# Three low parts of h made by GpSimd instead of VectorE in a split-precision graph kernel

## The reference

```python
h = maximum(layernorm(x, axis=-1), 0)          # (32, 256, 1024)
fv = h.mean(axis=1); nf = fv / norm(fv)        # graph from the column means
A  = adjacency(top_k(outer(nf, nf), 9)[1:])    # symmetric, ones on the diagonal, 1024 x 1024
t  = relu((A / deg) @ (h.T @ W1.T + b1))       # W1 = adj (256 x 256)
t  = (A / deg) @ (t @ W2.T + b2)               # W2 = adj as well
out = x + t.T
```

## Time and profile before

| | us |
|---|---|
| median of 3 runs | 477.64 (476.87 to 478.04) |
| the profiled execution | 475.69 |
| its span, first to last instruction | 473.9 |
| around the span | 1.79 |
| PE, DVE, ACT, POOL busy | 421.5, 395.6, 307.8, 220.9 |
| mean granted clock of TensorE | 0.986 of 2.4 GHz |

### The profile page before, as it was taken

How to read it: one execution, slowest core, us unless ns; L and a number is a source line. 1 busy time by engine, 2 the same in 40 slices (tenths; PEclk the granted TensorE clock), 3 DMA queues, 4 the chain that set the end, 5 groups by cost and what they waited for, 6 DMA issues and landing times.

```text
span 473.9 us, 7615 instructions
## 1 busy us (share of the span) xinstructions
PE 421.5 (89%) x2220; PEld 176.2 (37%) x2220; DVE 395.6 (83%) x682; ACT 307.8 (65%) x657; POOL 220.9 (47%) x937
## 2 busy tenths in 40 slices
PE   0653898999978799899999999899999999999996
PEld 0121343334323344344443443344434444344432
DVE  5999898988897998999899998999899828854463
ACT  2979687989766777667777769667766843014400
POOL 2536656374736435552737454744656253415200
PEclk9995999999999999999999999999999999999999
DMA  8990000159202493065703590078404400341026
GB/s 295 382 410 29 1 0 2 44 223 340 107 0 94 174 326 119 1 262 175 273 3 132 205 355 21 0 268 284 160 0 179 177 2 0 142 160 55 0 94 262
DMA packets 19401, 68.21 MB, mean 144 GB/s; under 512 B 1824, under 2 KB 2464, under 8 KB 19360
## 3 DMA queue, kind: packets, MB, share of 16 engines
q1 hardware_dynamic: 19360, 67.73, 38.2%
HBM read 34.17 MB, written 33.55 MB: 143 GB/s over the span
## 4 chain that ended last, share of the span: by engine, by line
DVE 39%; PE 31%; ACT 11%; issue 9%; POOL 7%; DMA 1%; POOLq 1%; SPq 0%; DVEq 0%; ACTq 0%
PE ps L451 26%; DVE hl L1109 9%; DVE hl L1118 7%; DVE bn L1087 7%; DVE xs L1134 5%; ACT hl L663 4%; ACT hf L654 4%; PE ps L457 3%; ACT hl L675 2%; DVE fv L1150 2%; DVE idx L1158 2%; POOL gat L876 2%; PE pm L506 1%; DMA xs<-x_dram 1%; POOL nw L858 1%
## 5 line engine op out<-in xcount | busy, mean ns | idle before, releaser
L451 PE MATMUL ps<-hl,wh 128*128 128x512 f16 x896 | 268.7, 382 | 20.6 <-DVE wl L1293 11.3
L451 PE MATMUL ps<-hl,wl 128*128 128x512 f16 x448 | 170.5, 381 | 0.0
L451 PEld LDWEIGHTS ps<-hl,wh 128*128 128x128 f16 x896 | 83.9, 99 | 131.4 <-issue 22.0
L654 ACT ACTIVATE hf<-xs,nbias,rstd 128x1024 f32<-128x1024 f32 x64 | 79.2, 1237 | 25.3 <-POOL nbias L862 17.4
L1109 DVE TENSOR_TENSOR hl<-hf,hl 128x1024 f16<-128x1024 f32 x64 | 76.9, 1211 | 15.5 <-ACT hl L663 15.3
L1134 DVE SCALAR_TENSOR_TENSOR xs<-ps,sc,xs 128x1024 f32<-128x1024 f32 (+1 forms) x71 | 78.9, 1137 | 5.9 <-PE ps L457 5.9
L1118 DVE SCALAR_TENSOR_TENSOR hl<-ps,hl 128x1024 f16<-128x1024 f32 (+1 forms) x55 | 57.2, 1083 | 20.3 <-ACT hl L675 20.2
L675 ACT ACTIVATE hl<-ps 128x512 f16<-128x512 f32 x96 | 55.7, 594 | 22.0 <-PE ps L457 22.0
L663 ACT ACTIVATE hl<-hf 128x1024 f16<-128x1024 f32 x64 | 67.6, 1056 | 2.0
L1087 DVE BATCH_NORM_STATS2 bn<-xs 128x6 f32<-128x512 f32 x96 | 61.2, 678 | 5.0 <-DMA xs<-x_dram 5.0
L451 PEld LDWEIGHTS ps<-hl,wl 128*128 128x128 f16 x448 | 44.0, 98 | 53.5 <-issue 1.1
(11 more groups left out here) (146 smaller groups left out, 537.6 us busy)
## 6 DMA issues: line engine op xcount, KB each, us to landing
xs<-x_dram SPq DMA_DIRECT2D x62, 512.0 KB, 7.4
out_dram<-xs SPq DMA_DIRECT2D x31, 1024.0 KB, 5.1
xs<-x_dram SPq DMA_DIRECT2D x4, 256.0 KB, 3.7
out_dram<-xs SPq DMA_DIRECT2D x4, 256.0 KB, 2.1
wt<-adj_t_dram SPq DMA_DIRECT2D x1, 256.0 KB, 9.8
b1r<-b_row_dram SPq DMA_DIRECT2D x1, 128.0 KB, 9.3
b2r<-b_row_dram SPq DMA_DIRECT2D x1, 128.0 KB, 10.8
cs<-consts_dram SPq DMA_DIRECT2D x1, 84.5 KB, 9.6
```

Of the source, the lines that this page charges most:

```text
L451: pe.matmul(bank(i, e), w[:, k, o], src, start=(k == 0 and w is wh and part == 0), stop=False)
L654: act.activation(hf[:, c % NHF], xs[:, n % NX, k], ACT.Relu, bias=nbias[:, n % RB, k:k + 1], scale=rstd[:, n % RB, k:k + 1], accum_out=s_a ...
```

## The change

The subtraction that makes the low part goes to GpSimd for three of the 64 chunks: (4, 1), that is batch 4, k = 1, then (5, 0) and (8, 0). The first two belong to group 1 and stand ahead of the first class rows, the third behind them. They are taken out of VectorE's list. Since `lo_ready` counts chunks and two engines now add to it, GpSimd waits until the chunk before is counted, and VectorE does so where the chunk before was GpSimd's.

```diff
+        ON_POOL = ((4, 1), (5, 0), (8, 0))
...
+            def pool_lo(n, k):
+                c = KC * n + k
+                pool.wait_ge(hi_ready, c + 1)
+                pool.wait_ge(lo_ready, c)
+                pool.tensor_tensor(hl[:, n % NHL, 1, k], hf[:, c % NHF], hl[:, n % NHL, 0, k], ALU.subtract
+                                   ).then_inc(lo_ready, 1)
...
             for n in range(6):
                 coefs(n)
+            pool_lo(4, 1)
             for b in batches(0):
                 gather(b)
             plain_q1(0)
+            pool_lo(5, 0)
             coefs(6)
             class_q1(0)
...
             late_sums(0)
+            pool_lo(8, 0)
             for b in batches(1):
                 gather(b)
...
                 dve.wait_ge(hi_ready, c + 1)
+                if ((c - 1) // KC, (c - 1) % KC) in ON_POOL:
+                    dve.wait_ge(lo_ready, c)
...
             kinds(0)
-            h_lo(4, 1)
             top_sums(0)
...
-            h_lo(5, 0)
             y_lo(*unit(0, 0)[1:])
             y_lo(*unit(0, 1)[1:])
...
             final(*unit(0, 11)[1:])
-            h_lo(8, 0)
             final(*unit(0, 12)[1:])
```

## The result

The changed kernel takes 480.5 us (median of 12 runs, 479.1 to 481.8) where the kernel before took 477.1 beside it (12 runs, 475.5 to 478.5). The ratio is 1.0082, with a 95% interval of 1.0068 to 1.0097: slower by 3.9 us, 3.2 to 4.6. The two medians alone differ by 3.4 us, which lies inside that interval. The profiled execution took 480.66 us, its span 478.9.

The account below looks back on a forecast made before the run. PE was busy for 89% of the span, but only the first two groups' handover, chained through GpSimd, counted. 2.75 + 1.35 - 0.1 + 0.6 = +4.6 us made 475.69 into 480.3, as median 482.2 us; range 479.4 to 484.2.

Parts of the forecast that it names:

- Term A: At chunk (4, 1): GpSimd waits for (4, 0), then subtracts, so gathers and VectorE's sum come late; +2.75 us.
- Term B: At chunk (5, 0): VectorE, making `cr`, stands until GpSimd's subtraction ends, so `lw` is late and PE waits; +1.35 us.
- Rival (1): At `cr` and layer 2's rows: VectorE is not held by GpSimd's long read; +2.5 us, 480.1 us; chance 0.24.
- The removal of (5, 0): VectorE no longer runs this chunk, but its next step needs ScalarE's read of the unit; -0.1 us.
- Term C: At chunk (8, 0): VectorE held at layer 2's rows, +0.8, less 0.2 gained behind the gathers; +0.6 us.
- Rival (2): PE's clock falls in the new gap before the first class rows; +0.9, in all +5.5 us, 483.1 us; chance 0.16.

Follow-up runs that it names:

- e4_mid41: The changed kernel with (4, 1) moved behind two of the four gathers of group 0, all three chunks still on GpSimd; 479.0 us, ratio 1.0059.
- e2_only50: The change cut to chunk (5, 0) alone on GpSimd, the other two back on VectorE; 477.3 us, ratio 1.0014 to the kernel before.
- e6_pieces50: Chunk (5, 0) alone on GpSimd, as eight subtractions of 128 columns instead of one; 476.7 us, ratio 1.0002 to the kernel before.
- e8_80late: Chunk (8, 0) alone on GpSimd, started only when `lw` of layer 2 is written; 476.2 us, ratio 0.9998 to the kernel before.
- e7_41filler: Chunk (4, 1) alone on GpSimd, with twelve unused matmuls filling PE's stop ahead of `plain_rows(0)`; 479.1 us, ratio 1.0044 to the kernel before.
- e3_only80: The change cut to chunk (8, 0) alone on GpSimd, the other two back on VectorE; 477.2 us, ratio 1.0005 to the kernel before.
- e1_only41: The change cut to chunk (4, 1) alone on GpSimd, the other two back on VectorE; 480.5 us, ratio 1.0080 to the kernel before.
- e5_filler: The changed kernel with twelve unused matmuls filling PE's stop ahead of `plain_rows(0)`; 481.3 us, ratio 1.0085 to the kernel before.
- e9_steady: The kernel before, with one chunk in each of groups 2 to 6 on GpSimd, behind `class_q1`; 474.5 us, ratio 0.9937.
- e11_two80: e10 with chunk (8, 0) also on GpSimd, started behind `lw` of layer 2 of group 0; 472.0 us, ratio 0.9903 to the kernel before.
- e10: e9_steady with a second chunk on GpSimd in groups 2 to 5, ahead of `late_sums`; 471.6 us, ratio 0.9887 to the kernel before.

## Why the prediction was right

**Term A**, 2.75 us by the prediction, measured 2.36. The order of events was as told: GpSimd stood for chunk (4, 0), then subtracted, then copied. The price was 2.13 us (2.1 predicted, from rows of 8 and 96 elements). What was too large is the stretch from there to the end of the gathers: 1.23 for the kinds and four batches of 1.23 make 6.15 us to the end of the last `hu` row, and it took 5.68 (46.18 to 51.86), a batch taking 1.17 and the kinds holding the copies for 1.0. e4_mid41 splits the term: 1.42 us are the place ahead of the gathers, 0.94 the work itself, less what GpSimd no longer stands for.

**Term B**, 1.35, measured 1.14 to 1.17. Rival (1), that VectorE is not held, is out: e2_only50 shows it standing until the subtraction ends, and e6_pieces50 shows that the hold goes with GpSimd's running instruction. The step was wrong in the instruction that stands. It is the TENSOR_SCALAR of 128x64, one tensor as input, ahead of the TENSOR_TENSOR that the prediction named. The section of the Trainium skill that the prediction cited (SBUF — State Buffer, "Who interferes with whom") covers this case as well: it counts `tensor_scalar` among the instructions that can enter a mode with both ports and then contend, when their operands meet certain conditions. The long row of `cr` agrees with it (1.45 for 0.26 us), and the two long rows with two inputs agree with what the prediction cited (2.10 for 1.23, 1.11 for 0.47 us). That this instruction ran in such a mode is what the page would say; the runs show only that it stood.

**The removal of (5, 0)**, -0.1, was worth 0.03 (1.17 at `lw`, 1.14 behind it): ScalarE is the cover, as said; VectorE waits 1.23 us for it there.

**Term C**, +0.6, measured 0.45 to 0.5. The hold of line 1242 was 0.64 us (0.8 predicted), shown by its absence in e8_80late. The time that is won when VectorE doesn't run (8, 0) was there too, 0.49 us, but it is worth nothing at the end, where the prediction gave it 0.2. The prediction misread its source: of the copies' delay only the 0.30 us of 1.38 against 1.08 came from (8, 0), and the idle time ahead of them (1.09) is still 1.06 in e8_80late, without it. What it missed is the wait that takes the gain up: e8_80late has it at PE until `plain_rows(1)`, and loses it where VectorE waits for ScalarE's `kind`, as the changed kernel also does (0.35 us).

**Rival (2), the clock,** came true beside the forecast and not instead of it. The prediction had it cost 0.9 us; it cost 0.5 in the whole change and 1.67 with (4, 1) alone. That A and B were 0.6 us smaller than told and the clock 0.5 us dearer is why the first class rows came 4.04 us late where 4.1 was forecast: that agreement is chance. It also means that the costs don't add: (4, 1) alone and the whole change are equally late there, since PE at half its clock covers what (5, 0) costs. The fall of this first clock was seen in the one profile that each of the two kernels has.

**The end.** The parts alone, from e7_41filler, e2_only50 and e3_only80, make 2.37 + 1.14 + 0.5 = 4.0 us without the clock, 4.5 with its first fall; the runs give 3.9 (3.2 to 4.6) and can't choose between them. The forecast was 4.6 over the profiled execution. Its median of 482.2 is 1.7 above the 480.5 measured: 0.7 of that is 4.6 for 3.9, 0.6 is that the kernel before had a median of 477.64 in three runs and of 477.1 in twelve beside the change, and the rest is that the two medians are only 3.4 us apart. So 480.5 as a number is nearer to rival (1)'s 480.1 than to the forecast; against rival (1) stand the held rows, and the 3.9 us (3.2 to 4.6) measured side by side, where it had 2.5.

**What stays open.** The second fall of the clock, at 135 to 142. It is seen in five profiles (the change, e1_only41, e5_filler, e9_steady, e11_two80) and not in e2, e3, e4, e6, e7, e8 and e10, behind a stop of PE of about 2.1 us there that the kernel before has too (2.15 us), with its clock kept in its profile. It cost the change 1.05 us in the profile and is no part of the 4.0. Being late there is not needed for it: e9_steady and e11_two80 were less than 0.4 us late. Each kernel has only one profile, and the mean clock that is on record for the other executions (0.972 to 0.989) doesn't say where the clock was low, so how often the fall comes is not known.

## What to carry to other kernels

Work that is given to a less busy engine should be put where that engine waits for others, not where others wait for it: nine chunks moved in the steady groups gained 5 us, three moved around the first class rows lost 4, and the busy shares of the kernel before, which are the same for both, can't tell the two apart. Ask of each moved instruction what it waits for in its new place (here 1.4 of 2.4 us), what is queued behind it, and which instruction of the neighbour runs at that time and may stand for it. A delay that makes TensorE stop can cost more than itself, since the clock may fall behind the stop, and then a second delay in its shadow may cost nothing at that point; so undo parts one at a time and also together.

## What the runs showed of the hardware

- VectorE stands for a running GpSimd subtraction of 128x1024 until it ends: 1.45 us for a TENSOR_SCALAR of 128x64 from float32 to float16 that takes 0.26 (the change), 3.00 us for a SCALAR_TENSOR_TENSOR of 128x1024 that takes 1.23 (e4_mid41). With pieces of 128 columns on GpSimd it stands for one piece, 0.53 us (e6_pieces50). MATCH_REPLACE8 beside such a subtraction took the same 1.21 or 1.22 us as elsewhere.
- A float32 and a float16 input to a float16 output of 128x1024 cost GpSimd 2.13 us, VectorE 1.22 and eight pieces on GpSimd 3.30 together.
- Behind a stop of PE of 2.8 us the clock fell in the one profile of each kernel that had it (the change, e1_only41), and it did not where the stop was filled; behind one of 2.1 us it fell in five of thirteen profiles, at 0.6 to 1.5 us each time.
